# Four edge stages of a graph network on one core: 32 hit matrices made ahead of the wait that all engines share

## What is computed

```python
# L0, two layers: gather rows of the source, weigh them, sum them per target
msg = x[src] * ew[:, None]
agg = segment_sum(msg, dst, num_segments=n) + x
neigh = agg / (count(dst) + 1)
out = x @ Ws.T + bs + neigh @ Wn.T + bn + bias;  x = where(out > 0, out, 0.2 * out)
# L1: sums of x[dst] per src, mean, two products, relu
# L2: sums of edge_attr per dst, two-layer network with layer norm and silu
# L3, two layers: reflect the gathered row at the unit vector of the edge's type, sum per target, mean
h_ref = h_src - 2.0 * sum(h_src * h_rel) * h_rel
out = segment_sum(h_ref, tgt) / max(deg, 1);  out = layer_norm(out @ W.T + x)
```

## Time and profile before

| | |
|---|---|
| time, median of 3 runs | 4401.65 us (4396.96 to 4405.56) |
| span of the profiled execution | 4783.9 us |
| mean granted TensorE clock | 0.898 |
| busy: TensorE, VectorE, ScalarE, GpSimd | 3733.3, 3413.8, 2211.2, 2954.6 us |
| stages behind a node phase begin at | l0b 1278.7, l1 2003.7, l3a 3310.9, l3b 3989.8 us |
| VectorE idle until the stage begins | 2.25, 5.25, 5.93, 2.89 us |

### The profile page before, as it was taken

How to read it: one execution, slowest core, us unless ns; L and a number is a source line. 1 busy time by engine, 2 the same in 40 slices (tenths; PEclk the granted TensorE clock), 3 DMA queues, 4 the chain that set the end, 5 groups by cost and what they waited for, 6 DMA issues and landing times.

```text
span 4783.9 us, 90087 instructions
## 1 busy us (share of the span) xinstructions
PE 3733.3 (78%) x18662; PEld 2281.7 (48%) x18662; DVE 3413.8 (71%) x13249; ACT 2211.2 (46%) x4608; POOL 2954.6 (62%) x3411
## 2 busy tenths in 40 slices
PE   2155799998778999777899999995678774778776
PEld 1012344477523455422598888894224442234443
DVE  5338965355665577743498988897877888768898
ACT  0000046733225688633366666664145652256666
POOL 4650355366566699866466666664665776656787
PEclk6556899999889999889899999997899997999999
DMA  3340157777524788534555555552456773467776
GB/s 88 99 74 6 53 173 222 251 230 232 168 86 159 246 259 271 175 124 130 170 166 161 167 162 161 161 168 66 122 180 227 235 234 113 147 194 246 226 238 194
DMA packets 536159, 810.98 MB, mean 170 GB/s; under 512 B 129245, under 2 KB 184005, under 8 KB 535709
## 3 DMA queue, kind: packets, MB, share of 16 engines
q1 hardware_dynamic: 318844, 532.13, 35.3%
q10 hardware_dynamic: 162769, 169.41, 10.5%
q0 software_dynamic: 54096, 104.47, 8.0%
HBM read 493.49 MB, written 311.41 MB: 168 GB/s over the span
## 4 chain that ended last, share of the span: by engine, by line
PE 47%; DVE 19%; issue 14%; DVEq 6%; POOL 6%; DMA 3%; another core or an unknown queue 2%; ACT 1%; POOLq 0%; ACTq 0%; SPq 0%; PEldq 0%
PE ps L1554 18%; DVEq L68 5%; DVE stat L1122 4%; PE ps L1719 4%; PE ps L1700 4%; PE ps L1701 4%; DVE hit L1071 3%; PE ps L1487 3%; POOL got L719 2%; PE ps L1679 2%; POOL x2T L734 2%; PE ps L1710 2%; PE ps L1680 2%; DVE mv L1128 2%
## 5 line engine op out<-in xcount | busy, mean ns | idle before, releaser
L754 POOL TENSOR_TENSOR rstd<-vare,neg_half 128x4 f32<-128x4 f32 x686 | 710.3, 1035 | 430.6 <-DVE vare L1135 429.6
L1554 PE MATMUL ps<-hit,got 128*128 128x512 bf16 x1172 | 492.5, 420 | 381.7 <-issue 155.9
L1316 ACT ACTIVATE evac<-ps 128x512 f32<-128x512 f32 x392 | 233.4, 595 | 861.8 <-PE ps L1554 625.3
L719 POOL DMA_INDIRECT got<-nodes_l,sorted_by_dst x392 | 398.2, 1016 | 239.5 <-PE ps L1554 109.8
L1554 PE MATMUL ps<-hit,tail 128*128 128x512 bf16 x1172 | 490.2, 418 | 22.8 <-issue 20.8
L1554 PE MATMUL ps<-hit,rest 128*128 128x512 bf16 x1172 | 491.9, 420 | 20.2 <-issue 18.9
L1163 DVE TENSOR_TENSOR nT<-sums,ps 128x512 f32<-128x512 f32 x392 | 268.9, 686 | 270.8 <-PE ps L1599 100.3
L1301 ACT ACTIVATE ps<-zeros 128x512 f32<-128x512 f32 x588 | 344.3, 598 | 195.0 <-DVEq L428 170.1
L1554 PEld LDWEIGHTS ps<-hit,got 128*128 x1172 | 121.8, 104 | 649.3 <-issue 566.0
L719 POOL DMA_INDIRECT got_pair<-in_x,sorted_by_dst x196 | 203.5, 1038 | 363.5 <-DVEq L428 190.1
L669 POOL DMA_INDIRECT records_by_src<-record,place_src x196 | 201.1, 1026 | 162.0 <-PE ps L1587 90.6
(11 more groups left out here) (276 smaller groups left out, 10298.4 us busy)
## 6 DMA issues: line engine op xcount, KB each, us to landing
nodes_l<-xout SPq DMA_DIRECT2D x196, 256.0 KB
xin<-nodes_l SPq DMA_DIRECT2D x196, 256.0 KB
sums<-sums_l SPq DMA_DIRECT2D x196, 256.0 KB
sums_l0a<-evac_pair ACTq DMA_DIRECT2D x98, 256.0 KB
sums_l<-evac_pair ACTq DMA_DIRECT2D x98, 256.0 KB
sums<-sums_l0a SPq DMA_DIRECT2D x98, 256.0 KB
sums_l0b<-evac ACTq DMA_DIRECT2D x98, 256.0 KB
sums<-sums_l0b SPq DMA_DIRECT2D x98, 256.0 KB
```

The costliest lines, as they stand in the source:

```text
L719: pool.indirect_dma_start(out=BUFFERS[name].got[0][:, k % RING, :], out_offset=None, in_=table, in_offset=bass.IndirectOffsetOnAxis(ap=sor ...
L754: pool.tensor_tensor(rstd[:, n, at, :], vare[:, n, at, :], neg_half[:, :], ALU.pow)\
L1316: act.activation(w.evac[h][:, slot, :], ps[:, BANKS * h + g % BANKS, :], ACT.Copy).then_inc(s["out"].sem, 1)
L1554: last = pe.matmul(into, part.rearrange("p a d -> p (a d)"), w.hit[:, i % w.hits, :], start=False, stop=False, skip_group_check=True)
```

## The change

VectorE's `edges` gets an argument `behind`. Where it is given, VectorE signs off the node phase itself, waits for one counter of that phase, makes the first 32 hit matrices, and only then waits for the common wait; `hits(32)` behind it then finds them made. l0a, which follows no node phase, is as before. For l0b the counter is the turned rows of all groups of d0, for l1 the sums with x added of d1, for l3a the turned rows of d2, for l3b the products of d3a. `nodes` on VectorE goes; every `stage_end(dve)` that it made is still there, at the same place of the stream. The other engines are untouched.

```diff
-            def edges(name, n):
-                stage_begin(dve, n)
+            def edges(name, n, behind=None):
                 s = edge_s[name]
...
+                if behind:
+                    stage_end(dve)
+                    dve.wait_ge(*behind)
+                    hits(32)
+                stage_begin(dve, n)
                 hits(32)
                 for b in range(BATCHES):
                     dve.wait_ge(*s[f"got{b % 4}"](64 * (b // 4 + 1)))
...
-            def nodes(phase):
-                phase()
-                stage_end(dve)
-
             edges("l0a", 1)
-            nodes(d0)
-            edges("l0b", 2)
-            nodes(d1)
-            edges("l1", 3)
-            nodes(d2)
-            edges("l3a", 4)
-            nodes(lambda: d3("d3a", 0))
-            edges("l3b", 5)
-            nodes(lambda: d3("d3b", 1))
+            d0()
+            edges("l0b", 2, node_s["d0"]["tx"](GROUPS))
+            d1()
+            edges("l1", 3, node_s["d1"]["add"](GROUPS))
+            d2()
+            edges("l3a", 4, node_s["d2"]["tx"](GROUPS))
+            d3("d3a", 0)
+            edges("l3b", 5, node_s["d3a"]["mm"](GROUPS))
+            d3("d3b", 1)
+            stage_end(dve)
```

## The result

The changed kernel took 4409.64 us (median, 4404.95 to 4416.62) beside 4402.31 us for the kernel before (4392.53 to 4409.83); the ratio is 1.0017, interval 1.0011 to 1.0024. That is 7.3 us slower (4.8 to 10.6), where 8.9 us faster was forecast. The time lies 2.6 us above the range.

A forecast was written before the change was run, and what follows sets the result against it. No one engine bounds the whole, but the start of each stage is VectorE's. Gains of 9.4 us at four seams less 0.5 us for tails give 8.9 us off 4401.65: 4392.7 us, range 4382 to 4407.

The forecast's parts named there:

- The seams are VectorE's: At four stage starts VectorE idles 2.25, 5.25, 5.93 and 2.89 us, then makes 32 hits before touching the first batch.
- When VectorE is free: At the four seams, hits started in the idle time would end at 1286.56, 2008.14, 3314.73 and 3996.60 us.
- Its fourth gather ends on GpSimd at ..., and this does not move, since GpSimd still waits for the seam: First batch of each stage: its fourth gather stays at 1283.68, 2008.75, 3316.01 and 3994.84 us.
- Gathers beside hits show nothing of it (0.94 us in all four stages): At the stage starts, gathers running beside VectorE's hits were taken to be undisturbed, at 0.94 us each.
- The rule that was weighed against the change and set aside: Skill page: tensor_scalar can lock VectorE and GpSimd out mutually; by it the d1 and d2 seams lose up to 1.2 us.
- The tails of d1 and d2: Hits beside GpSimd's last power and multiplication cost 0.25 us in each phase, 0.5 together, bounds 0 and 1.2.
- The head start and its size: VectorE touches the first batch earlier by 2.1, 3.0, 2.2 and 2.1 us in l0b, l1, l3a and l3b.
- case A: Whole kernel: the head start lasts, the stall being a length, not a date; 4389 to 4397 us, chance 0.54.
- The stalls: VectorE's "issue" stops over 20 us into l1, l3a and l3b, 1.04, 4.91 and 8.37 us, read as late code.
- B: Stalls are dates: l3a and l3b give nothing, l0b and l1 half; 4398 to 4402 us, chance 0.22.
- C: Slower: GpSimd's pause in l1 shortens, gathers follow on, VectorE's stall grows 5 us; 4404 to 4412 us, chance 0.13.
- D: Missing code is requested earlier, so part of the l3a and l3b stalls goes; 4377 to 4387 us, chance 0.11.

The follow-up runs named there:

- e4: The kernel before, with GpSimd waiting for the fourth hit before its first gather in four stages: 4424.32 us, ratio 1.0051.
- e1: The changed kernel with the new waits kept but all 32 hits put back behind the common wait: 4403.07 us, ratio 1.0005.
- c0_same: The kernel before, unchanged, run and profiled once more as a control: ratio 1.0001, profiled span 4402.8 us.
- e2: The changed kernel with only 8, 18, 20 and 9 hits ahead of the common wait, the rest behind it: 4393.78 us, ratio 0.9986.
- e5: The changed kernel with its first 16 hits per stage made by scalar_tensor_tensor, with two inputs in memory: one run of 4425.53 us.
- e3: The changed kernel, all 32 hits ahead, with a drain of VectorE behind every second one: 4381.37 us, ratio 0.9956.
- e9: The changed kernel with one single drain behind the 24th early hit: one run of 4397.96 us beside 4401.42.
- e6: The changed kernel with its first 16 hits per stage made by tensor_scalar on one input read in strides: one run of 4461.92 us.

## Why the prediction was wrong, point by point

**The seams are VectorE's (right).** The undisturbed profile repeats the idle times to 0.15 us, and e4 shows that what VectorE loses at its first batch the kernel loses.

**When VectorE is free (right).** The hits end 8.49 us after they start; the forecast had 9.7 to 10.1, as beside the gathers. The new wait costs nothing that can be measured (e1, within 0.9996 to 1.0014).

**"Its fourth gather ends on GpSimd at ..., and this does not move, since GpSimd still waits for the seam" (the step that failed).** GpSimd does begin at the seam, but its first gather ends with VectorE's stream. The fourth gather moves by what the first is longer, 6.0, 3.0, 2.0 and 5.5 us. This is where the 9.4 us went: the sum took the later of two ends, VectorE's hits and the gathers, as if the two ran side by side, and they run one behind the other. Put in their order, the case is: hits, then 0.9 us of the first gather, then three more at 1.25, then the landing. For l0b that is 1081.09 + 0.84 + 3 x 1.25 to the end of the fourth gather at 1085.7, and VectorE's start at 1087.34 is 1.65 us behind it. The lower end of the forecast for that step, 1.55 us, was right.

**"Gathers beside hits show nothing of it (0.94 us in all four stages)" (the reading that let it through).** The rows were right and proved less than they were asked to. They show gathers that follow on others, begun at the seam together with the hits. No seam of the kernel before has a gather that comes to a GpSimd at rest for 3.9 to 9.3 us while VectorE is two microseconds or more into a stream. The nearest rows lie within the stages, after rests of about a microsecond, and there a gather gets through; of l1 in c0_same:

```profile
1776.17 5.49 DVE L1071 TENSOR_SCALAR hit<-node_of,node_at_src 128x512 bf16<-128x512 f16 x18
1779.21 1.08 POOL L719 DMA_INDIRECT got<-nodes_a,sorted_by_src  x1 [0.89 <-PE ps L1554]
```

In c0_same no gather at all takes longer than 1.47 us, so the kernel before would not have given the hold-up away. A price of VectorE's they do show: beside gathers the 32 hits take 9.67 to 10.09 us, 0.30 to 0.31 us each, and the first profile has hits without a gather beside them too, at 0.265 us each:

```profile
3342.00 4.81 DVE L1071 TENSOR_SCALAR hit<-node_of,node_at_dst 128x512 bf16<-128x512 f16 x18
```

VectorE gives way by 1.2 to 1.6 us in 32 hits, some 0.15 to 0.2 for each of the eight gathers, one every 1.25 us, that run beside them. Two engines that slow each other down so share something, and this comparison was not made.

The rule that was weighed against the change and set aside was the one that pointed at the loss. The Trainium skill, "SBUF — State Buffer", section "Who interferes with whom", names the writing of gather descriptors as what GpSimd can't do meanwhile, and says that who issues first keeps the ports. The prediction asked only what GpSimd's arithmetic loses by it, and who profits when the hits leave the gathers' side. It did not ask what a stream that is already running at the seam does to the first gather. By rows: 6.99 us instead of 0.97.

**The tails of d1 and d2 (right).** 0.24 and 0.33 us; forecast 0.25 each.

**The head start and its size (right once the stream fits).** e2 has 2.5, 3.0, 2.9 and 2.8 us at the first batch, forecast 2.1, 3.0, 2.2 and 2.1, and 6.2 us (2.2 to 10.1) in time. So case A's mechanism, a head start that lasts, holds once the gather isn't held up, and how much of it lasts to the end is known only within that interval.

**The stalls (moot).** Rivals B, C and D all hang on the "issue" stops of rows 6. Those of l3a and l3b are absent in the undisturbed profile. C had the sign and even the size (4404 to 4412), by luck and not for its reason: there is no such stop to be made longer; that it "decides as soon as the head start in l1 reaches some 2 us" is refuted by e2, where it is 3.0 us and the kernel is faster. A span 382 us above the median of the runs was a reason to have the profile taken again before resting three rivals on two stops: the idle times at the seams repeated, and so did the stops of d3a, but those two did not.

**The rival that was missing.** With the forecast's own durations, and the first gather ending 0.9 us behind the hits (the one number that the first profile didn't show), the first batch is begun at the end of the hits + 0.9 + 3 x 1.25 + 1.55 us. From the seams of rows 2 the hits end at +7.84, +4.42, +3.82 and +6.79, so VectorE begins at +14.0, +10.6, +10.0 and +13.0, where it was +10.0, +9.6, +9.7 and +9.6: later by 4.0, 1.0, 0.4 and 3.4 us, 8.8 in sum, 9.3 with the tails. That is 4411 us, measured 4409.6. That it comes so close is in part luck: hits of 0.265 us instead of 0.31 bring the loss at the first batches near the measured 4.4 us, and the kernel lost more than these. It would have been the rival on the slower side, and its point of decision is where the stream's end passes the seam by some 3.5 us.

## What to carry to other kernels

Moving VectorE's work ahead of a wait lets it run when GpSimd comes back; the first gather behind the wait, if it arrives in the middle of an unbroken stream of VectorE, can pay for the whole rest of the stream. Cut the early work to the idle time, or break it with a drain every few instructions, and test a claim "the two don't disturb each other" against rows in which the one under question comes second and from rest. And where a change of a few instructions moves the time by more than its rows explain, compare the stages that it doesn't touch: the same loop cost 335 or 319 us by where VectorE's code lay.

## What the runs showed of the hardware

- A gather (L719, one indirect DMA of GpSimd) has a median of 0.95 us and at most 1.47 us in c0_same. The first gather of a stage takes 0.97 to 1.12 us there and in e1, but up to 7.48 us if an unbroken stream of ordinary hits has been running for 1.96 us or more (e4 and the change), and 18.02 us behind strided ones; it ends 0.74 to 0.98 us behind the end of the stream, or 0.87 us behind a drain in it. GpSimd's small power does the same: 19.79 us instead of 1.01, though its row begins 0.44 us ahead of the hits.
- A first gather 0.24 us behind the first hit gets through (0.97 us), one 1.96 us behind it doesn't (7.38). The point at which it turns over was not tried. Why two gathers got through the two-input hits of e5 (1.26 and 1.47 us) and two didn't (10.13 and 9.76) stays open.
- Gathers that are flowing mostly aren't held up by hits; the seventh gather of l0b in e5 was (4.53 us). Within the stages it goes both ways: in l1, with GpSimd at rest for 1.1 to 1.3 us and the stream 2.7 us old, a gather took 1.09 us in the changed kernel and 2.37, 2.47, 2.50 and 2.50 us in e1, e3, e4 and e9. What decides there is open.
- A drain frees the gather (e9, e3). Going through the common wait does in e2 and e6 and doesn't in l1 and l3a of e5; no idle time shows in the timeline in l0b and l3b of e2, nor in e5 and e6.
- Empty instructions, 48 in one place, were worth 15.6 us in one loop and cost 10.0 in the next.
